# Two attention blocks: the output projection in three float32r passes over both tiles, with O^T and Wo split, and a new order of the group

## The reference, cut to what matters

```python
def _attn(xq, xc, Wq, Wk, Wv, Wo, bo):
    q = (xq @ Wq).reshape(B, N, HEADS, D_HEAD)      # HEADS 16, D_HEAD 64
    k = (xc @ Wk).reshape(B, S, HEADS, D_HEAD)
    v = (xc @ Wv).reshape(B, S, HEADS, D_HEAD)
    scores = jnp.einsum('bnhd,bshd->bhns', q, k) * scale
    attn = jax.nn.softmax(scores, axis=-1)
    out = jnp.einsum('bhns,bshd->bnhd', attn, v).reshape(B, N, HEADS * D_HEAD)
    return out @ Wo + bo                             # Wo is 1024 x 128
x = _attn(_ln(x, g1, b1), _ln(x, g1, b1), Wq1, Wk1, Wv1, Wo1, bo1) + x    # phase SELF
x = _attn(_ln(x, g2, b2), context, Wq2, Wk2, Wv2, Wo2, bo2) + x           # phase CROSS
```

## Time and profile before

| | |
|---|---|
| median of 3 runs | 487.98 us |
| lowest and highest | 485.27 and 488.25 us |
| the profiled execution | 491.05 us |
| its span, first to last instruction | 489.3 us |
| mean granted TensorE clock | 0.986 |

### The profile page before, as it was taken

The page is one execution under the profiler, slowest core; times in us unless marked ns, Lnnn a source line. Parts: engine busy times, 40 slices in busy tenths (PEclk is TensorE's granted clock), DMA queues, the critical chain, the costliest instruction groups (busy, mean ns, idle before and its releaser), DMA issues.

```text
span 489.3 us, 17734 instructions
## 1 busy us (share of the span) xinstructions
PE 465.1 (95%) x7688; PEld 421.9 (86%) x7688; DVE 362.3 (74%) x652; ACT 278.5 (57%) x505; POOL 193.7 (40%) x218
## 2 busy tenths in 40 slices
PE   8699899999999999999999999989999899989997
PEld 8688798888999998989989888878998677778897
DVE  4588688878887787788878877785874676887462
ACT  4465644645657557566555474554464576764673
POOL 4635452333324623743444235332442131330473
PEclk9999999999999999999999999989999799998999
DMA  7750000000000000000000000000000000000011
GB/s 234 188 163 5 1 3 3 1 4 3 1 3 11 3 11 8 4 12 1 11 11 1 12 9 4 3 1 2 1 0 17 9 17 11 0 3 1 1 43 45
DMA packets 17301, 10.58 MB, mean 22 GB/s; under 512 B 7888, under 2 KB 16272, under 8 KB 17232
## 3 DMA queue, kind: packets, MB, share of 16 engines
q1 hardware_dynamic: 16800, 9.48, 7.1%
q10 hardware_dynamic: 432, 0.07, 0.1%
HBM read 8.50 MB, written 1.05 MB: 20 GB/s over the span
## 4 chain that ended last, share of the span: by engine, by line
PE 85%; DVE 8%; issue 4%; DMA 1%; ACT 1%; ACTq 0%; POOL 0%; DVEq 0%
PE out0p L753 13%; PE stage L569 12%; PE stage L570 11%; PE stage L571 11%; PE scp L661 7%; PE scp L703 6%; PE scp L862 6%; PE stage L736 4%; PE scp L736 4%; DVE mx L1136 3%; PE out0p L767 3%; PE scp L677 2%; DMA bias<-in_L_xattn_bo_dram 1%; DVE vb L1113 1%; PE stage L785 1%
## 5 line engine op out<-in xcount | busy, mean ns | idle before, releaser
L1375 POOL TENSOR_TENSOR pr<-pr,rc 128x1024 f32<-128x1024 f32 x32 | 60.3, 1905 | 72.2 <-DVE rc L1161 72.2
L939 ACT ACTIVATE pr<-pr 128x1024 f32<-128x1024 f32 x48 | 50.6, 1055 | 54.5 <-DVE pr L1131 51.4
L753 PE MATMUL out0p<-wo_of,ot 128*128 128x128 f32 x512 | 65.7, 281 | 0.6 <-issue 0.6
L753 PEld LDWEIGHTS out0p<-wo_of,ot 128*128 128x128 f32 x512 | 59.6, 191 | 2.9 <-issue 0.8
L1126 DVE TENSOR_REDUCE mx<-scp 128x16 f32<-128x1024 f32 x32 | 39.2, 1224 | 20.9 <-PE scp L661 20.9
L883 ACT ACTIVATE vt<-stage 64x512 f32<-64x512 f32 x64 | 37.9, 592 | 29.5 <-PE stage L571 27.9
L883 ACT ACTIVATE q_of_heads<-stage 128x512 f32<-128x512 f32 x64 | 34.8, 599 | 33.6 <-PE stage L571 33.2
L661 PE MATMUL scp<-k_of_heads,q_of_heads 64*64 64x64 f32 x2048 | 38.6, 221 | 9.1 <-issue 8.2
L1166 DVE COPY vt<-stage 64x512 f32<-64x512 f32 x64 | 44.4, 694 | 2.5 <-PE stage L571 0.6
L661 PEld LDWEIGHTS scp<-k_of_heads,q_of_heads 64*64 64x64 f32 x2048 | 34.2, 134 | 12.1 <-issue 9.2
L1105 DVE COPY k_of_heads<-stage 128x512 f32<-128x512 f32 x32 | 22.1, 692 | 26.0 <-PE stage L571 26.0
(11 more groups left out here) (235 smaller groups left out, 1324.5 us busy)
## 6 DMA issues: line engine op xcount, KB each, us to landing
ctx_in<-in_ctx_dram SPq DMA_DIRECT2D x16, 96.0 KB, 2.0
wo_of<-in_L_xattn_Wo_dram SPq DMA_DIRECT2D x2, 512.0 KB, 9.5
out_dram<-rows SPq DMA_DIRECT2D x8, 128.0 KB, 1.8
rows<-in_x_dram SPq DMA_DIRECT2D x1, 768.0 KB, 9.7
pr<-in_L_xattn_Wq_dram SPq DMA_DIRECT2D x1, 512.0 KB, 4.5
pr<-in_L_xattn_Wk_dram SPq DMA_DIRECT2D x1, 512.0 KB, 6.5
pt<-in_L_xattn_Wv_dram SPq DMA_DIRECT2D x1, 512.0 KB, 7.7
rows<-in_L_xattn_Wq_dram SPq DMA_DIRECT2D x1, 512.0 KB, 8.3
```

Of the source, the lines that this page charges most:

```text
L753: last = nc.tensor.matmul(out0p[:, t * D:(t + 1) * D], ot[:, a // 2, a % 2, t, :], wo_w[s.phase][:, a, :], start=(a == 0), stop=(a == PAIR ...
L939: nc.scalar.activation(pr[t][:, :], pr[t][:, :], ACT.Exp, scale=scale[s.phase]).then_inc(exped, 1)
L1375: nc.gpsimd.tensor_tensor(halves(pr[t][:, :]), halves(pr[t][:, :]), rc[:, t, :, None].to_broadcast([ROWS, H, N]), ALU.mult).then_inc(probs, 1)
```

## The change

- Wo is a product of three float32r passes over both tiles at once. Wo is split into a high part and a rest (`wo_s`), made by ScalarE (`high_out_step`) and GpSimd (`out_weight_step`) in groups SELF 0 and SELF 7, and lies in buffers that are free by then. O^T is split as well: ScalarE copies each bank of `av` into `ot_h`, and VectorE subtracts that from the same bank into `ot_r`. Wo is now the stationary operand and O^T of both tiles the moving one, 256 columns wide, so the product comes out turned; ScalarE copies it (`out_step`), and TensorE turns it back (`out_turn_step`).
- All four banks of `av` are now uses of the three `stage` banks, and each is released by ScalarE and VectorE both. Before, two were `scp` banks, and each was copied by one engine.
- All eight banks of `proj` are copied by ScalarE; before, VectorE copied two of them.
- The order of the group is new on every engine: on TensorE `av` of tile 0 and the last values, the scores of tile 0 of the next group, `x_step`, then `av` of tile 1, the scores of tile 1, two banks of projections, Wo of the group before, three banks, the turning back, three banks.

```diff
-    if kind == "proj":
-        return (0, 1) if i in PROJ_BY_DVE else (1, 0)
-    if kind == "val":
+    if kind in ("val", "av"):
         return 1, 1
-    if kind == "av":
-        return (1, 0) if i % 2 == 0 else (0, 1)
-    if kind in ("x", "qk", "at", "up1", "pt"):
+    if kind in ("proj", "x", "qk", "at", "up1", "pt"):
         return 1, 0
     return 0, 1
...
+            if before:
+                for i in (2, 3):
+                    self.use("av", before.phase, before.first, i)
             for t in range(T):
                 self.softmax(p, g, t)
             self.p(one.phase, one.first, (0, 1) if last else None)
-            for i in range(4):
+            for i in range(3):
                 self.use("val", p, g, i)
             for t in range(T):
                 self.turned(p, g, t)
             for i in (0, 1):
-                self.use("av", p, g, i, staged=False)
+                self.use("av", p, g, i)
+            self.use("val", p, g, 3)
             if last:
                 self.p(one.phase, one.first, (2, 3))
             self.x(two.phase, two.first)
-            for i in (2, 3):
-                self.use("av", p, g, i)
-            self.tick("out0", (p, g))
-            self.tick("added", (p, g))
+            if last:
+                for i in (2, 3):
+                    self.use("av", p, g, i)
+            for name in ("out_turned", "out_copied", "out0", "added"):
+                self.tick(name, (p, g))
...
+
+        def chunks_of(ap):
+            return ap.rearrange("p (a d) -> p a d", d=D)
+
+        wo_s = [[chunks_of(m[:, :]) for m in wp_s], [chunks_of(m[:, :]) for m in wq_s[SELF]]]
+        for p in (SELF, CROSS):
+            raw[p]["o"] = chunks_of(masked_k[:, p, :, :].rearrange("p h n -> p (h n)"))
+        outT = attT
...
-            if kind == "av" and i < 2:
-                return scp[:, i, :]
...
-            return ot[:, :, i, t, :], home("av", s, u)[:, :].rearrange("p (m n) -> p m n", m=PAIRS // 2)
+            return ot_h[:, :, i, t, :], home("av", s, u)[:, :].rearrange("p (m n) -> p m n", m=PAIRS // 2)
```

TensorE:

```diff
                 if t == 0:
                     pe.wait_ge(act, cnt.at("act", s, 7, kind="proj"))
-                    pe.wait_ge(dve, cnt.at("dve", s, PROJ_BY_DVE[-1], kind="proj"))
-                    if s.before():
-                        pe.wait_ge(act, cnt.at("act", s.before(), 0, kind="av"))
-                        pe.wait_ge(dve, cnt.at("dve", s.before(), 1, kind="av"))
...
             def av_step(s, t):
 
-                if t == 0:
-                    banks = [home("av", s, i) for i in range(2)]
-                else:
-                    banks = [stage_for(s, "av", s, 2 + i) for i in range(2)]
+                banks = [stage_for(s, "av", s, 2 * t + i) for i in range(2)]
...
-            def out_step(s, t):
+            def out_step(s):
 
                 before = s.before()
-                if t == 0 and before:
+                if before:
                     pe.wait_ge(added, cnt.at("added", before))
-                if t == 0 and s.turn is None and s.first == 0:
-                    pe.wait_ge(loaded_w[s.phase]["o"], 16)
-                pe.wait_ge(act, cnt.at("act", s, 2 * t, kind="av"))
-                pe.wait_ge(dve, cnt.at("dve", s, 2 * t + 1, kind="av"))
-                for a in range(PAIRS):
-                    last = nc.tensor.matmul(out0p[:, t * D:(t + 1) * D], ot[:, a // 2, a % 2, t, :],
-                                            wo_w[s.phase][:, a, :], start=(a == 0), stop=(a == PAIRS - 1))
-                if t == 1:
-                    last.then_inc(out0, 1)
+                if s.first == 0:
+                    pe.wait_ge(rest_o, 1 + s.phase)
+                wh, wr = wo_s[s.phase]
+                for i in range(2):
+                    pe.wait_ge(dve, cnt.at("dve", s, 2 + i, kind="av"))
+                    for m in range(PAIRS // 2):
+                        a = 2 * m + i
+                        mh, mr = (o[:, m, i, :, :].rearrange("p t r -> p (t r)") for o in (ot_h, ot_r))
+                        nc.tensor.matmul(out0p[:, 0:GR], wh[:, a, :], mh, start=(i == 0 and m == 0), stop=False)
+                        nc.tensor.matmul(out0p[:, 0:GR], wh[:, a, :], mr, start=False, stop=False)
+                        last = nc.tensor.matmul(out0p[:, 0:GR], wr[:, a, :], mh, start=False,
+                                                stop=(i == 1 and m == PAIRS // 2 - 1))
+                last.then_inc(out_turned, 1)
+
+            def out_turn_step(s):
+
+                pe.wait_ge(out_copied, cnt.at("out_copied", s))
+                for t in range(T):
+                    last = nc.tensor.transpose(out0p[:, GR + t * D:GR + (t + 1) * D], outT[:, t * ROWS:(t + 1) * ROWS],
+                                               ident[:, :])
+                last.then_inc(out0, 1)
...
-                    scores_step(s, 0)
                     if before:
-                        out_step(before, 0)
+                        av_step(before, 1)
                     scores_step(s, 1)
-                    if before:
-                        out_step(before, 1)
                     if last:
                         p_step(one, s, (0, 1))
                     else:
-                        proj_step(one, s)
+                        proj_step(one, s, range(2))
+                    if before:
+                        out_step(before)
+                    if not last:
+                        proj_step(one, s, range(2, 5))
+                    if before:
+                        out_turn_step(before)
+                    if not last:
+                        proj_step(one, s, range(5, 8))
                     val_step(s, (0, 1))
                     turn_step(s, 0)
                     val_step(s, (2,))
                     turn_step(s, 1)
+                    av_step(s, 0)
                     val_step(s, (3,))
-                    av_step(s, 0)
                     if last:
                         p_step(one, s, (2, 3))
+                    else:
+                        scores_step(one, 0)
                     x_step(two, s)
-                    av_step(s, 1)
                     if last:
-                        out_step(s, 0)
-                        out_step(s, 1)
+                        av_step(s, 1)
+                        out_step(s)
+                        out_turn_step(s)
...
+            scores_step(Step(SELF, 0), 0)
```

ScalarE:

```diff
             def av_step(s, t):
-                sc.wait_ge(full, cnt.at("full", s, 2 * t, kind="av"))
-                copy(*av_copy(s, 2 * t)).then_inc(act, 1)
+                for i in range(2):
+                    sc.wait_ge(full, cnt.at("full", s, 2 * t + i, kind="av"))
+                    copy(*av_copy(s, 2 * t + i)).then_inc(act, 1)
+
+            def out_step(s):
+
+                sc.wait_ge(out_turned, cnt.at("out_turned", s))
+                copy(outT[:, :], out0p[:, 0:GR]).then_inc(out_copied, 1)
+
+            def high_out_step(p):
+
+                sc.wait_ge(loaded_w[p]["o"], 16)
+                copy(wo_s[p][0], raw[p]["o"]).then_inc(high_o, 1)
...
-                    last = one.phase == GEGLU
+                    before, last = s.before(), one.phase == GEGLU
+                    if before:
+                        av_step(before, 1)
+                    exp_step(s, 0)
                     if last:
-                        exp_step(s, 0)
                         exp_step(s, 1)
+                        out_step(before)
                         load_table(ACT.Gelu)
                         p_step(one, (0, 1))
                     else:
-                        exp_step(s, 0)
-                        p_step(one, (0,))
+                        p_step(one, range(2))
                         exp_step(s, 1)
-                        p_step(one, range(1, 8))
+                        if before:
+                            out_step(before)
+                        p_step(one, range(2, 8))
                     val_step(s, (0, 1))
                     pt_step(s, 0)
                     val_step(s, (2,))
                     pt_step(s, 1)
+                    av_step(s, 0)
                     val_step(s, (3,))
-                    av_step(s, 0)
                     if last:
                         p_step(one, (2, 3))
                     x_step(two)
                     if s.is_group(SELF, 0):
+                        high_out_step(SELF)
                         high_step(CROSS, "q", high_cross)
+                    if s.is_group(SELF, GROUPS - 1):
+                        high_out_step(CROSS)
                     if s.is_group(SELF, 1):
                         high_step(CROSS, "k", high_cross)
                     if s.is_group(SELF, GROUPS - 2):
```

VectorE:

```diff
-                    for i in which:
-                        if i not in PROJ_BY_DVE:
-                            continue
-                        ve.wait_ge(full, cnt.at("full", s, i, kind="proj"))
-                        nc.vector.tensor_copy(*proj_copy(s, i)).then_inc(dve, 1)
```

(41 more changed lines are left out.)

22 lines of the change are left out of this document (9 added, 13 removed).

## The result

The changed kernel took 496.06 us (median of 4 runs, 495.64 to 496.3) against 488.12 us before in the same comparison: ratio 1.0165, 95% interval 1.0113 to 1.0218. It is slower by more than 1%; the forecast was 487.0, with a range up to 495.

The account below looks back on a forecast made before the run. TensorE, busy 95% of the span, was taken as the bound. Groups 0, weights +3.0, stalls -5.5 and last group +1.5 gave -1.0 us: 490.05 profiled, 487.0 median; own range 483 to 491.5, with rivals 477 to 495.

Parts of the forecast that it names:

- GpSimd's work moves behind its scaling: Each group: GpSimd's rows are wanted only at x_step, some 3 us later, so the move has no cost.
- Last group of CROSS: End of CROSS: nothing covers copy and subtraction ahead of Wo, some idle hidden by Wo; -2 to +3, taken as +1.5 us.
- it lies 3.07 above the median: Step from profiled execution to median: 491.05 against 487.98 before, so 490.05 forecast becomes a median of 487.0.
- The product: Wo on TensorE: 24 rows in 2.9 us instead of 3.79 us; net -0.52 us a group with turning back.
- Turning back: TensorE, after the Wo product: two transposes, 0.37 us a group.
- The wait for VectorE: SELF groups: TensorE waits 0.54 us for VectorE's release of av banks, plus about 0.1 to start again; group 19.17 us.
- First rival: Banks come free in time and TensorE alone sets the pace: 479 us (475.5 to 482.5), chance 0.31.
- Second rival: Longer run of 64-row pieces makes nearly every group stall by 0.8 us: 495 us (491.5 to 499), chance 0.16.
- Stalls: TensorE's instruction waits in the scores: six of 0.4 us left, 2.3 us; -5.5 us, bounds -7.8 to +4.5.
- The third rival: Instruction stalls don't heed the order and stay: median 492.5 us, chance 0.06.
- The first stall: Instruction stall behind the first scores, 3.3 us at a time of heavy loading, left as it is.
- Weights: ScalarE making a weight's high part after x_step delays av copies in certain groups: 0 to 4.0, taken as +3.0 us.

Follow-up runs that it names:

- that run: Changed kernel with GpSimd signalling x's rest before the context's, so CROSS q projections wait for x's alone: 493.36 us, ratio 1.0061.
- the run with the three passes alone: Kernel before with O^T split and Wo in three passes, turned back behind the fifth projection bank, all else in its old order: 494.37 us, ratio 1.0085.
- The shifted run: Kernel before with each warm-up product cut into two of 64 columns, so later TensorE instructions stand further down its list: 506.28 us, ratio 1.0324.
- the edits together: Changed kernel with stage banks waited for last, q waiting for x's rests only, last values copied by ScalarE alone, last group reordered: 488.57 us, ratio 0.9973.

## Why the prediction was wrong

The forecast fell at two steps of its sum, both on work whose cover I named without measuring it, and at the step from the sum to the median.

"GpSimd's work moves behind its scaling, and its rows are wanted only at x_step, some 3 us later; no cost." Its normalized rows are wanted at x_step, but its rests are wanted by the projections that follow. The diff moved x_step from 7.5 us ahead of these to 2.6 us, and the chain through ScalarE and GpSimd takes 3.8. I gave a CROSS group 19.17 and it took 19.80. 0.52 of these 0.63 us go with the context's rest, 8 x 0.52 = 4.2 us; the other 0.11 stays in that run, where the wait for VectorE is the only one left.

"Last group of CROSS ... I take +1.5", measured +4.8 like for like: 3.3 us. The chain at its end cost what I had for it, 1.51 for the subtraction ahead of Wo and 0.47 for the turning back. What I left out are the waits ahead of it: for the up-projection's bank (0.61), for turning back a second time (0.47), ahead of the product with values of tile 1 (0.86), and 0.84 more of issue waits. I also took part of the present idle as hidden by Wo; the wait for hid went from 1.99 to 2.12 instead.

"The profiled execution took 491.05, so 490.05; it lies 3.07 above the median": I carried the offset of one slow execution over to a kernel whose executions differ by 0.7 us in all (495.64 to 496.3). That is 3.0 of the 9.1 us.

Point by point for the rest:
- The product: 24 rows in 2.88 us (2.9 forecast). Turning back adds 0.2, not 0.37, so the product saves 0.70 and not 0.52.
- The wait for VectorE: forecast 0.54 + 0.1 a group of SELF. It came to 0.77 + 0.13, and 19.05 - 0.70 + 0.90 = 19.25 is the group that was measured (19.24; 19.17 forecast). So two misses, 0.18 and 0.26, nearly offset each other. VectorE's copy ended 2.76 us after the product of tile 0 (2.7 forecast); the miss is the restart, 0.37 from its end to TensorE's product, where I had 0.1. A wait with one semaphore behind it costs 0.15 (136.16 to 136.31 in the run with the three passes alone). Four waits stand behind the late one; at 0.055 each they would make up the rest, which was only argued.
- First rival (banks come free in time): refuted. Second rival (stalls in nearly every group): refuted, three issue waits of 1.77, 1.65 and 1.27. It gave nearly the measured time by a mechanism that did not happen.
- Stalls: -5.5 forecast, -5.5 measured, or -4.6 with the last group. That the size came out is no proof of its reason. The shifted run halves the stalls with the old order; up to GEGLU the three versions with the old order have 8.8, 10.2 and 4.4 us of issue waits, the ten with the new one 4.2 to 9.2. Among those ten, the ones in which TensorE waits less for other engines have the most (7.4 to 9.2), which would fit the prediction's reason, that such waits give a delivery time; it is not separated from the place in the list. The third rival is not refuted. The first stall, 3.26 us, which the prediction left as it is, came to 1.77. The Trainium skill, Runtime: NRT & Kernel Launch, section Instruction fetch mechanics, calls block crossings mostly hidden; the shifted run, with its 4.4 us of stalls that moved with the place in the list, agrees with the blocks and not with "mostly".
- Weights: +3.0 forecast, +0.9 measured (0.69 in SELF 0 and 0.19 in SELF 6). In CROSS the wait for GpSimd was longer and hid them; with that wait gone they showed 0.46 to 0.48 each, not 0.85.

## What to carry to other kernels

When a step moves, follow its results to their last consumer and compare the length of that whole chain, from a group where nothing waits, with the time that the new place leaves; the profile of before has both numbers. When a profiled execution lies off its median, first see whether the offset belongs to the kernel or to that execution: others of the same kernel, with their granted clocks, tell. When a step saves time on the busiest engine and adds a link to the release of its buffers, work out the release at each place where it is used, the last iteration too, for there nothing covers it. When several waits overlap, removing the longest shows the next; the edits together gave more than each alone. And a sum that comes out right says little about its reason when a mere shift of the list changes it as much.

## What was not expected of the hardware

- A wait instruction that is already fulfilled still took 0.055 us of TensorE (four of them 0.22).
- A row of a float32 product of 64 columns took as long as one of 128, 0.22 us each in the first warm-up (48 rows in 10.50 us, against 24 in 5.49), and with the halved products TensorE kept that pace until 26 us.
- Behind TensorE's wait of 2.12 us the granted clock was 0.74, 0.50 and 0.90 in the next three steps of 2 us (326 to 332 us), so in part at the lower of its two levels (1.2 GHz); with that wait at 0.87 it stayed at 1.00.
- A wait was put down to ScalarE's xT, which had nothing to do with it: the copy of VectorE that the product reads ended later by the timeline, and the run that gave this copy to ScalarE halved the wait.
